# A four-block transformer kernel: five moves in the hand-written order of work

## What is computed

```
t_sa, t_ca, t_mlp = split(silu(t_emb) @ tp_w + tp_b, 3)
x = x + mha(ln1(x), ln1(x)) + t_sa[:, None, :]
x = x + mha(ln3(x), context, mask) + t_ca[:, None, :]
x = x + gelu(ln2(x) @ w1 + b1) @ w2 + b2 + t_mlp[:, None, :]
```

```
sh_sa, sc_sa, g_sa, sh_ff, sc_ff, g_ff = split(silu(t_emb) @ adaln_w + adaln_b, 6)
x = x + g_sa * attend(ln(x) * (1 + sc_sa) + sh_sa)
x = x + attend(ln(x), context)
x = x + g_ff * (gelu((ln(x) * (1 + sc_ff) + sh_ff) @ fc1_w) @ fc2_w)
```

## Time and profile before

| | us |
|---|---|
| median of 3 runs | 3945.83 |
| lowest and highest of them | 3935.78, 3947.87 |
| the profiled execution, its own time | 3947.87 |
| its span from first to last instruction | 3946.1 |
| PE busy, share of the span | 3578.6, 91% |
| DVE busy | 2221.8, 56% |
| ACT busy | 2326.0, 59% |
| POOL busy | 846.3, 21% |
| mean granted TensorE clock | 0.951 |

### The profile page before, as it was taken

How to read it: one execution, slowest core, us unless ns; L and a number is a source line. 1 busy time by engine, 2 the same in 40 slices (tenths; PEclk the granted TensorE clock), 3 DMA queues, 4 the chain that set the end, 5 groups by cost and what they waited for, 6 DMA issues and landing times.

```text
span 3946.1 us, 65974 instructions
## 1 busy us (share of the span) xinstructions
PE 3578.6 (91%) x20057; PEld 2080.2 (53%) x20057; DVE 2221.8 (56%) x3560; ACT 2326.0 (59%) x4082; POOL 846.3 (21%) x550
## 2 busy tenths in 40 slices
PE   7999997999899988999898979998999889899988
PEld 5776774346534744347435743464346443563366
DVE  3333335853585547833775458536854477538654
ACT  2333335775477446764675557755774567557764
POOL 3322222005200511024003410051024100330051
PEclk8998998998999889999999999999999899999999
DMA  3001102000000110010000010100001100100010
GB/s 132 20 13 33 32 1 75 1 28 23 22 2 12 34 44 1 2 39 33 1 2 23 23 44 2 39 23 12 2 12 33 44 1 18 33 22 1 2 34 23
DMA packets 70785, 92.81 MB, mean 24 GB/s; under 512 B 9227, under 2 KB 57934, under 8 KB 70350
## 3 DMA queue, kind: packets, MB, share of 16 engines
q1 hardware_dynamic: 40958, 63.40, 4.8%
q10 hardware_dynamic: 29520, 25.39, 2.1%
HBM read 77.96 MB, written 9.50 MB: 22 GB/s over the span
## 4 chain that ended last, share of the span: by engine, by line
issue 79%; POOL 17%; PE 3%; DVE 1%; POOLq 0%; ACT 0%; DMA 0%; SPq 0%; ACTq 0%; DVEq 0%
POOL hidl L1784 3%; PE ps L640 3%; POOL hidl L1819 3%; POOL x L1810 2%; POOL ql L1837 2%; POOL small L1744 2%; POOL kl L1837 1%; POOL hTl L1751 1%; POOL W2l L1830 1%; POOL W2h L1828 1%; POOL W1h L1828 1%; DMA sel_in<-in_sel 0%; DVE tok L1436 0%; PE ps L1101 0%; POOLq L1836 0%
## 5 line engine op out<-in xcount | busy, mean ns | idle before, releaser
L1385 ACT ACTIVATE probs<-ps 128x512 f32<-128x512 f32 (+1 forms) x2176 | 1188.1, 636 | 364.0 <-PE ps L640 363.6
L1706 DVE TENSOR_REDUCE mxh<-ps 128x2 f32<-128x1024 f32 x1024 | 1205.6, 1220 | 250.0 <-PE ps L640 248.4
L640 PE MATMUL ps<-probs,v 128*32 128x512 f32 (+1 forms) x4864 | 658.4, 614 | 6.3 <-ACT probs L1385 6.3
L640 PE MATMUL ps<-qs,ks 64*128 64x512 f32 x2048 | 610.1, 476 | 0.0
L640 PEld LDWEIGHTS ps<-qs,ks 64*128 64x128 f32 x2048 | 260.6, 185 | 563.2 <-ACT probs L1385 465.1
L1744 POOL TENSOR_TENSOR small<-small 128x4 f32<-128x4 f32 x66 | 68.2, 1034 | 1812.0 <-DVE small L1430 1812.0
L640 PE MATMUL ps<-ks,qs 64*128 64x512 f32 x2048 | 382.1, 438 | 77.5 <-DVE mxh L1706 61.3
L640 PEld LDWEIGHTS ps<-ks,qs 64*128 64x128 f32 x2048 | 192.3, 185 | 236.6 <-DVE mxh L1706 180.4
L640 PE MATMUL ps<-hT,slot 128*128 128x512 f32 x448 | 235.7, 660 | 21.4 <-ACT hT L1168 9.2
L1703 DVE TENSOR_REDUCE mx<-ps 128x4 f32<-128x312 f32 x384 | 167.2, 478 | 145.8 <-PE ps L640 142.2
L640 PE MATMUL ps<-slot,hT 128*128 128x256 f32 x896 | 225.0, 398 | 9.3 <-ACT hT L1396 9.3
(11 more groups left out here) (222 smaller groups left out, 6171.2 us busy)
## 6 DMA issues: line engine op xcount, KB each, us to landing
slot<-in_L_w SPq DMA_DIRECT2D x8, 1024.0 KB, 6.9
slot<-in_L_fc_w SPq DMA_DIRECT2D x8, 1024.0 KB, 5.2
adw<-in_L_adaln_w SPq DMA_DIRECT2D x4, 1536.0 KB, 6.5
xin<-in_x ACTq DMA_DIRECT2D x5, 1024.0 KB, 5.6
x_after_block<-x ACTq DMA_DIRECT2D x20, 256.0 KB, 2.3
xin<-x_after_block ACTq DMA_DIRECT2D x5, 1024.0 KB, 5.4
ew<-in_L_e_w SPq DMA_DIRECT2D x6, 768.0 KB, 12.3
x<-in_x ACTq DMA_DIRECT2D x4, 1024.0 KB, 7.4
```

Of the source, the lines that this page charges most:

```text
L640: return pe.matmul(out, lhsT, rhs, start=start, stop=stop)
L1385: ins = act.activation(dst, src, ACT.Exp, scale=SCALE)
L1706: dve.tensor_reduce(mxh[:, z, t, j // 2, j % 2, :], ps[:, a:a + 2, :], AX.X, ALU.max, negate=True).then_inc(dve_done, M.add(dve_done, name))
```

## The change

1. In the fill of both self attentions `beside` becomes one step for each of the 16 gaps between maxima. The maxima no longer come in twos at the start, `K q 1 0` uses all 128 rows of the array, and the first half of `K k 1 1` moves behind the sixteenth `A`.
2. `V 1` leaves the fill; `V 1`, `V 2`, `V 3` come in units 0, 1, 2 instead of the fill, unit 0 and unit 1. `R` and `add` move from unit 4 into its place. `R` takes one bank instead of two, and the split of the banks begins with the first `S` instead of with the 17th `A`.
3. `R` of L1mlp moves from the lead of L1ca to behind `T 0` of L1mlp, and goes to `rrow` instead of `grow`. So SP loads `W2` later, and `split W2` of L1mlp moves on POOL from L1ca to behind `up 1 1` of L1mlp. `mod` of L2 moves from between the two `T` of L1mlp to behind `up 1 4`.
4. In L2mlp `R` comes ahead of `N 1`.
5. In L3ca `K dddd k 0 0`, `K adad k 1 0` and `R` come earlier in the lead.

```diff
-        q01, k10, q10, q11, k11 = (halves("q", 0, 1), halves("k", 1, 0), halves("q", 1, 0), halves("q", 1, 1, "A"), halves("k", 1, 1, "A"))
-        beside = [[], [("P", "k", 1, 0)], q01, [], [("P", "q", 1, 1)], k10, [], [("P", "k", 1, 1)], q10[:1], q10[1:], q11[:1], q11[1:], [],
-                  k11[:1], [], []]
+        beside = ([("P", "k", 1, 0)] + halves("q", 0, 1) + [("P", "q", 1, 1)] + halves("k", 1, 0) + [("P", "k", 1, 1)]
+                  + [w for k in halves("q", 1, 0, "A") + halves("q", 1, 1, "A") for w in (k, None)] + halves("k", 1, 1, "A"))
...
-            put(tag, *beside[i])
+            put(tag, *[w for w in beside[i:i + 1] if w])
         more(first_slot + 1)
-        put(tag, *k11[1:], ("V", 1))
+        put(tag, *beside[first_slot:], ("R",), ("add",))
...
-            if u < 2:
-                put(tag, ("V", u + 2))
+            if u < 3:
+                put(tag, ("V", u + 1))
...
-            if u == 4:
-                put(tag, ("R",), ("add",))
...
             put(tag, ("N", 1), ("K", "aaaa", "q", 0, 0), then, ("R",))
-            if tag == "L1ca":
-                put("L1mlp", ("R",))
         else:
-            put(tag, ("T", 0), *projections("k", 0), ("N", 1), first, then, ("T", 1), ("K", "dddd", "k", 0, 0), ("K", "aaaa", "q", 0, 0),
-                ("P", "q", 0, 1))
+            put(tag, ("T", 0), *projections("k", 0), ("N", 1), first, ("K", "dddd", "k", 0, 0), then, ("T", 1), ("K", "aaaa", "q", 0, 0),
+                ("K", "adad", "k", 1, 0), ("P", "q", 0, 1), ("R",))
...
-            put(follow, ("split", "W1"), ("split", "W2"))
+            put(follow, ("split", "W1"), *[("split", "W2")] * (follow == "L2mlp"))
...
-        put(follow, ("T", 0), ("N", 1), *[("R",)] * (follow == "L2mlp"))
-        if follow == "L1mlp":
-            put("L2sa", ("mod",))
-        put(follow, ("T", 1), *[("up", 0, m) for m in range(FM)])
+        put(follow, ("T", 0), ("R",), ("N", 1), ("T", 1), *[("up", 0, m) for m in range(FM)])
...
-        put(tag, ("add",), ("up", 1, 0), ("up", 1, 1), *[("up", 1, m) for m in range(2, 5)])
-        put(follow, *[("mod",)] * (follow == "L3ca"))
+        put(tag, ("add",), ("up", 1, 0), ("up", 1, 1), *[("split", "W2")] * (tag == "L1mlp"), *[("up", 1, m) for m in range(2, 5)])
+        put(follow, ("mod",))
...
+                stack_maxima("L1ca")
                 sp.wait_ge(mm_done, upto(mm_done, ("row", "L1mlp")))
                 sp.dma_start(W2, wide(T["L1_w2"])).then_inc(slot_loaded[3], M.add(slot_loaded[3], "L1mlp", LOADED))
-                stack_maxima("L1ca")
...
-                        count = 2 if kind in ("A", "R", "OT") else 1
-                        if TPH * GH <= asked[tag] < GROUPS * NH * TPH * GH:
+                        count = 2 if kind in ("A", "OT") else 1
+                        if tag in begun and asked[tag] < GROUPS * NH * TPH * GH:
```

More of the change, by code:

```diff
@@ L237, in cross_attention @@
         else:
-            put(tag, *maxima[:2], ("K", "adad", "k", 1, 0), *maxima[2:4], ("K", "AAAA", "q", 1, 0), *maxima[4:6], ("P", "q", 1, 1), *maxima[6:8],
-                ("R",), *maxima[8:10], ("V", 0))
+            put(tag, *maxima[:4], ("K", "AAAA", "q", 1, 0), *maxima[4:6], ("P", "q", 1, 1), *maxima[6:10], ("V", 0))
         put(tag, *maxima[10:14], ("K", "aaaa", "q", 0, 1), *maxima[14:16])
@@ L871, in _ @@
             used = [0] * 7
-            asked = {t: 0 for t in KIND}
+            begun, asked = set(), {t: 0 for t in KIND}
             M.open("blocks")
@@ L918, in single @@
                         if not alone:
+                            if kind == "S":
+                                begun.add(tag)
                             return shared(kind)
@@ L1619, in _ @@
                             dve.wait_ge(mm_done, upto(mm_done, ("row", tag)))
-                            dve.tensor_copy(grow[:] if tag == "L1mlp" else rrow[:], ps[:, M.where(("row", tag)), 0:D]
-                                            ).then_inc(dve_done, M.add(dve_done, ("row", tag)))
+                            dve.tensor_copy(rrow[:], ps[:, M.where(("row", tag)), 0:D]).then_inc(dve_done, M.add(dve_done, ("row", tag)))
                         if tag == "L1sa":
@@ L1809, in _ @@
                         pool.wait_ge(dve_done, upto(dve_done, ("row", tag), (ln, "xh", NT - 1)))
-                        pool.tensor_tensor(x[:], xin[:] if tag == "L1sa" else x[:], (grow if tag == "L1mlp" else rrow)[:].unsqueeze(1).to_broadcast([P, NT, D]), ALU.add
+                        pool.tensor_tensor(x[:], xin[:] if tag == "L1sa" else x[:], rrow[:].unsqueeze(1).to_broadcast([P, NT, D]), ALU.add
                                            ).then_inc(pool_done, M.add(pool_done, ("row", tag)))
```

## The result

The changed kernel takes 3971.85 us (median of 7 runs, 3951.25 to 3984.63) against 3941.28 us (7 runs, 3935.78 to 3947.87): the ratio is 1.0073, with a 95% interval of 1.0047 to 1.0097. A second set gave 3971.49 against 3939.94, 1.0070 (1.0043 to 1.0097). It is slower by 0.7%, where 3944 was forecast and 3966 was the upper end.

The account below looks back on a forecast made before the run. DVE's reduces of the maxima were taken to bound the self attentions, PE the MLP. Terms summing to -0.4 us a pass, -1.6 in four, carried to the median of 3945.83, gave 3944 us; 8-in-10 range 3919 to 3966.

Parts of the forecast that it names:

- self attention: L1sa and L2sa, fill and first units: -1.1 us each, -2.2 us for the two in a pass.
- L2mlp: Second transposes in L2mlp: with the copies first, the normalisation runs after POOL's `hTl`, -0.3 us a pass, bounds -1.5 and +1.
- L3ca: Lead of L3ca: shorter row of maxima cancels against a wait for ACT's copies, -0.3 us a pass, bounds -2 and +2.5.
- Net -0.3 until unit 1 begins: Each self attention, from `M` to unit 1: `V` leaves, `R` comes, the second `S` waits for a reduce; -0.3 us net.
- `V` in unit 2: Unit 2 of each self attention: a `V` beside its `PV` costs nearly the whole `V`, +1.95 us.
- `R` out of unit 4: Unit 4 of each self attention: without `R` only DVE's usual pause of 0.26 us stays, -3.0 us.
- `R` out of L1ca's lead: L1ca, ahead of maxima whose stacks were ready: PE no longer does `R` there, -2.1 us a pass, bounds 0 and -4.
- L1mlp: L1mlp up to the first `o`: start 3.3 us earlier, `mod` costs 5.0, PE waits 2.7 for POOL; +4.5 us a pass.
- a sign of being wrong: In L1mlp, the forecast would be wrong if the first `o` waited for nothing; it expected PE idle about 2.7 us.
- A: Rival: in the self attentions' fill the clock stays up and most of the wait goes, 3 us more each; 3920 us, chance 0.20.
- B: Rival: the fill brings nothing and the wait ahead of `o 0` in L1mlp lowers the clock, +1.7 us; 3960 us, chance 0.24.
- C: Rival: PE reaches `o 0` last, so L1mlp costs +1.7 us a pass instead of +4.5; 3933 us, chance 0.12.

Follow-up runs that it names:

- the run with both limits lifted: The changed kernel with the split of `W2` done by DVE instead of POOL and `mod` in bank 6, which no `up` step uses: 3955.99 us, ratio 1.0036 against the kernel before.

## Why the prediction was wrong

Its forecast of the sum was -1.6 us; the runs say +28. By part, as each alone measured, and with `mod`'s bank taken out of the first: self attention +14 (forecast -8.8), the MLP's part with `R` out of L1ca and L2mlp +4 (forecast 4 x (-2.1 + 4.5 - 0.3) = +8.4), L3ca +10 (forecast -1.2). They sum to +28. Each of these is uncertain by about 7 to 12 us, by the intervals of the ratios, and `mod` waits for its bank in the whole but not in the MLP's part alone, so that they meet the 28 so closely is in part luck.

**The step that failed** is "Net -0.3 until unit 1 begins". I had seen that the second `S` takes the bank of a maximum and waits for its reduce, and priced it as a wait among others. Two things were missing. The maxima stand behind that `S` and the `V` in PE's queue, so PE's wait empties DVE, the engine that sets the pace there. And the lower clock follows: `V` took 3.47 us for 1.99.

The stretch from `M` to unit 1 can be compared over profiles. In the five with the new order and the new rule (both of the changed kernel and three experiments) it took 13.41 us in L1sa and 14.41 in L2sa; in the five with the old order and the old rule 11.74 and 11.63. So the step forecast at -0.3 measured +1.7 and +2.8 us, in four passes some 18 us where -2.4 was forecast. That is 20 of the 30 us between forecast and result. In the three with the new order and the old rule it took 11.62 and 10.88 us, -0.1 and -0.8: there the forecast would have held. The eight self attentions as a whole took 1941.8 us (1931.9 to 1946.5), 1929.7 and 1915.0 us (1913.2 to 1917.3) in these three groups: 12 us more than before, and 27 more than the same order with the old rule. The first profile of the changed kernel hid a part of it, with +0.7 and +2.3 us. And the range of the prediction held bounds of costs from one execution, not the spread of the clock from one execution to the next.

**What held.** `M` came 23.5 us after the first `A` in L1sa (23.7 forecast, 24.2 before). `V` in unit 2: +1.92 (+1.95). `R` out of unit 4: -3.3 (-3.0). `R` out of L1ca's lead: 5.95 to 3.83, -2.1 as forecast. But the whole stage L1ca was 3.0 us a pass shorter, and 3.7 us in the mean of the seven profiles without that `R` against the seven with it. The prediction saw nothing to be won there beyond `R`. `split W2` had left the stage in the same seven, and the two were not tried apart. The first `up` came 5.43 us behind the start of `R` (5.0), DVE's second normalisation took 1.37 us (1.38).

**L1mlp: the sum right, a term wrong.** +5.3 us in a pass against +4.5. But PE did not wait 2.7 us for POOL. The first `o` waited for nothing, which the prediction had named as a sign of being wrong: `mod` cost 6.2 us with its bank wait, not 5.0, the `up` steps behind it 2.5 more, and POOL was done 1.3 us earlier. POOL's bound was real, though, as the part alone shows (`W2l` released the first `o`).

**L3ca**: I let the wait for ACT's copies cancel against stacks and `R` that leave the row of maxima. The first wait was 1.2 us; what was missed is that the stacks then come one by one at the pace of ACT's copies (2.38 us for 1.10) and that the clock falls behind them, to 0.50 (`R` 1.22 us for 0.69). L2mlp was +0.6 instead of -0.3; its cause was not tried.

**The rivals.** A (3920) counted on the clock staying up because the wait of 1.74 us goes; the new order made a wait of its own, as the argument against it said. Its first half came: from `M` to the first `S` the clock stayed at 1.00, where it had been 0.75. The rule of the Trainium skill that stood beside A (TensorE: Matmul & The Clock Gate, "What's actually happening": the throttled state is the default, activity releases it) agrees with these rows, where the clock falls behind a wait (0.55 in the `V` of 3.47 us, behind the wait of 1.82), but it told nothing of which order has the longer wait. B (3960) is nearest: slower, by the lower clock, but it looked for it ahead of `o 0`. C did not come: PE was last at `o 0`, but only by having lost more.

## What to carry to other kernels

When a change alters which buffer a step gets, walk the rotation before and after, and ask for each new wait what stands behind it in the queue and which engine that starves. A wait of 1.8 us on the busiest engine cost 1.5 us more by the lower clock in one profile and over 3 us in another, and 1.70 us in another order cost nothing by it; so take such prices from several executions. And a step that belongs to another stage (`mod`, `R`) should have its buffer chosen by hand: `mod` in a free bank is worth 25 us by itself, more than any of the five moves.

## What the hardware showed

Three things were new to me. The mean granted clock moved between 0.943 and 0.953 over executions of one program on one core, and the time with it by 36 us. The stretch ahead of the first pass took about 624, 631 to 634 or 638 us, whatever the kernel. And in the run with both limits lifted the clock fell behind a `mod` (3.63 us) that had waited for nothing; by its records PE was busy throughout. The windows of `mod`, and of the `up` steps behind it up to the first `o`:

```profile
1821.00:1825.40 4.40, 4.40 (x36) 4.16 (x35) 0.36 (x4) 1.40 (x3) 4.40 (x3) 0.98 0.00 0
1825.40:1830.30 4.90, 4.90 (x16) 3.95 (x15) 0.00 (x0) 2.41 (x4) 4.90 (x5) 0.67 0.01 3
```

The granted clock goes from 0.98 to 0.67 without any wait of PE between them; here the fall of the clock had no idle stretch in PE's records ahead of it.
